# Who issues a 2 KB transfer: the shift row moves from SyncE's queue to ScalarE's, and its copies ahead of two exps

## The reference

```python
def _L0_conv_ref(x, Wq, bq, Wk, bk, Wv, bv):        # B=8, C=512, S=1024 tokens, 8 heads of 64
    t = x.reshape(B, C, S).transpose(0, 2, 1)
    q = t @ Wq.T + bq ; k = t @ Wk.T + bk ; v = t @ Wv.T + bv
    q = q.reshape(B * NUM_HEADS, S, hd)             # k and v likewise
    scores = jnp.einsum('gqd,gkd->gqk', q, k) / jnp.sqrt(hd)
    attn = jax.nn.softmax(scores, axis=-1)
    wv = jnp.einsum('gqk,gkd->gqd', attn, v)
...
x = x + _L0_conv_ref(_gn(x), ...)                   # _gn: group norm, 32 groups
x = x + _L1_conv_ref(_gn(x), ...)                   # mask, relu, 3x3 convolution, bias
```

## Time and profile before

| what | us |
| --- | --- |
| median of 3 runs (lowest, highest) | 2591.8 (2591.47, 2593.41) |
| the profiled execution | 2588.92 |
| its span, first to last instruction | 2587.1 |
| 100 to 1480 us, attention in its regular part: PE busy / DVE busy / ACT busy of 1380 | 1356.72 / 1092.56 / 760.76 |
| 1480 to 1830 us, attention's last slots, with the convolution's preparation | PE busy 326.88 of 350 |
| 1830 to 2587 us, convolution | PE busy 745.40 of 757 |

### The profile page before, as it was taken

How to read it: one execution, slowest core, us unless ns; L and a number is a source line. 1 busy time by engine, 2 the same in 40 slices (tenths; PEclk the granted TensorE clock), 3 DMA queues, 4 the chain that set the end, 5 groups by cost and what they waited for, 6 DMA issues and landing times.

```text
span 2587.1 us, 39690 instructions
## 1 busy us (share of the span) xinstructions
PE 2499.2 (97%) x11720; PEld 986.9 (38%) x11720; DVE 1936.6 (75%) x2647; ACT 1141.9 (44%) x2059; POOL 1124.8 (43%) x971
## 2 busy tenths in 40 slices
PE   6899999999999999999999999988999999999998
PEld 2333333333333333333333333332444444444443
DVE  5877787878788787887878888887676967967415
ACT  4455555455555555555555554456232132132100
POOL 1466467457556646655655664554112021030000
PEclk9999999999999999999999999999999999999999
DMA  5324243251433415323243332511444634633533
GB/s 159 84 71 118 69 128 87 61 138 55 123 84 98 117 44 130 102 69 106 71 122 83 109 106 58 136 48 60 173 177 152 238 133 176 228 130 131 209 113 149
DMA packets 209643, 300.66 MB, mean 116 GB/s; under 512 B 82192, under 2 KB 131472, under 8 KB 209424
## 3 DMA queue, kind: packets, MB, share of 16 engines
q1 hardware_dynamic: 209424, 297.97, 38.7%
HBM read 194.49 MB, written 52.69 MB: 96 GB/s over the span
## 4 chain that ended last, share of the span: by engine, by line
PE 86%; DVE 6%; issue 2%; ACT 2%; DMA 2%; POOL 1%; SPq 0%; DVEq 0%; ACTq 0%; POOLq 0%
PE bank L835 27%; PE bank L741 16%; PE bank L715 15%; PE bank L676 12%; PE bank L694 8%; PE bank L686 6%; DVE nmax L1264 2%; PE bank L704 1%; DMA q_b<-shift 1%; ACT prob L918 1%; DVE prob_sum L1258 1%; DVE bn L220 1%; PE bank L728 0%; DVE val L1276 0%; DVE xn L1334 0%
## 5 line engine op out<-in xcount | busy, mean ns | idle before, releaser
L1264 DVE TENSOR_REDUCE nmax<-bank 128x1 f32<-128x512 f32 x1024 | 657.6, 681 | 230.5 <-PE bank L694 226.2
L918 ACT ACTIVATE prob<-bank 128x512 f32<-128x512 f32 x1024 | 560.5, 593 | 502.7 <-PE bank L715 502.3
L835 PE MATMUL bank<-v,u_slab 128*128 128x512 f16 x3456 | 746.9, 379 | 0.0
L1093 POOL TENSOR_TENSOR prob_sum<-prob_sum,prob 128x512 f32<-128x512 f32 x354 | 504.6, 1425 | 369.0 <-ACT prob L918 368.1
L741 PE MATMUL bank<-prob,val 128*64 128x512 f32 x2048 | 495.9, 605 | 0.0
L835 PEld LDWEIGHTS bank<-v,u_slab 128*128 128x128 f16 x3456 | 338.1, 98 | 406.9 <-issue 0.8
L694 PE MATMUL bank<-k_a,q_a 128*128 128x512 f16 x1024 | 384.7, 383 | 18.4 <-DVE nmax L1264 10.3
L1258 DVE TENSOR_TENSOR prob_sum<-prob_sum,prob 128x512 f32<-128x512 f32 x354 | 353.4, 998 | 3.5 <-issue 0.3
L715 PE MATMUL bank<-q_a,k_a 128*128 128x512 f16 x1024 | 315.6, 381 | 18.0 <-ACT prob L918 16.4
L715 PE MATMUL bank<-q_b,k_b 128*128 128x512 f16 x1024 | 306.2, 381 | 9.5 <-DMA q_b<-shift 9.5
L741 PEld LDWEIGHTS bank<-prob,val 128*64 128x64 f32 x2048 | 124.1, 136 | 248.7 <-issue 206.8
(11 more groups left out here) (139 smaller groups left out, 2512.1 us busy)
## 6 DMA issues: line engine op xcount, KB each, us to landing
u_slab<-u_scratch SPq DMA_DIRECT2D x72, 1024.0 KB, 5.0
xs<-x SPq DMA_DIRECT2D x28, 1024.0 KB, 5.7
tile<-x_scratch SPq DMA_DIRECT2D x26, 1024.0 KB, 5.9
u_scratch<-u_w SPq DMA_DIRECT2D x96, 192.0 KB, 2.7
q_a<-qk_hi SPq DMA_DIRECT2D x64, 256.0 KB, 4.9
den_sb<-recip_scratch SPq DMA_DIRECT2D x128, 128.0 KB, 2.9
x_scratch<-xr SPq DMA_DIRECT2D x16, 1024.0 KB, 4.5
xr<-x SPq DMA_DIRECT2D x15, 1024.0 KB, 7.7
```

The source lines that it names most:

```text
L835: mm = pe.matmul(bank_at(pos, co)[:].rearrange("p (i n) -> p i n", i=2), slab[:, l, c, co * P:(co + 1) * P], image[v][:, 2 * c:2 * c + 2, ...
L918: act.activation(prob[:, (2 * u + e) % 8], sc_bank[bank_turn(s * 16 + 2 * u + e, 16 * HPI)[0]][:], ACT.Exp, scale=float(D) ** -0.5).then_i ...
L1093: nc.gpsimd.tensor_tensor(acc, in0, prob[:, (2 * kc + 1) % 8], ALU.add).then_inc(s1["sum1"], 1)
L1264: dve.tensor_reduce(nmax[:, m // 2, m % 2:m % 2 + 1], src[:], AX.X, ALU.max, negate=True)\
```

## The change

The transfer of the shift row is no longer issued by SP but by ACT, from its own DMA queue, right behind the four copies and after a wait for them (`shift_sent`). `send_shift` is gone. Beside that the copies, and with them the new wait and the new issue, move: where the slot has r < 3 they stand ahead of both exps of unit 6, where r = 3 they stay between them.

```diff
-            def send_shift(h, s):
-
-                half, tok = tokens(s)
-                sp.wait_ge(s1["shift_sent"], TOK // SQ * (h + 1))
-                sp.dma_start(q_b[half][D:D + 1, :, tok], shift[:]).then_inc(s1["shift_row"], 16)
...
-                if nxt:
-                    send_shift(img * HPI + s + 1, (s + 1) % HPI)
...
-            def gather_shift(h, first=False):
+            def gather_shift(h, s, first=False):
...
+                half, tok = tokens(s)
+                act.wait_ge(s1["shift_sent"], TOK // SQ * (h + 1))
+                act.dma_start(q_b[half][D:D + 1, :, tok], shift[:]).then_inc(s1["shift_row"], 16)
...
+                    if nxt and u == UNITS - 2 and r < HPH - 1:
+                        gather_shift(h + 1, (s + 1) % HPI)
                     exp_tile(h, s, u, 0, added)
-                    if nxt and u == UNITS - 2:
-                        gather_shift(h + 1)
+                    if nxt and u == UNITS - 2 and r == HPH - 1:
+                        gather_shift(h + 1, (s + 1) % HPI)
                     exp_tile(h, s, u, 1, added)
```

More of the change, by code:

```diff
@@ L559, in _ @@
             load_x(1, 0)
-            send_shift(0, 0)
             slot(0, 0, prev=False)
@@ L1045, in _ @@
                 qk_evacuate(1, 0, j)
-            gather_shift(0, first=True)
+            gather_shift(0, 0, first=True)
             slot(0, 0, prev=False)
```

## The result

| | before | changed |
| --- | --- | --- |
| median of the runs made together (lowest, highest) | 2592.45 us (2591.47, 2593.41), 4 runs | 2611.37 us (2609.9, 2614.28), 4 runs |
| again, with more rounds | 2591.34 us (2589.69, 2594.66), 9 runs | 2610.97 us (2610.12, 2613.9), 5 runs |
| span of the profiled execution | 2587.1 us | 2609.8 us |

The ratio is 1.0072 with a 95% interval of 1.006 to 1.0084, and 1.0078 (1.0064 to 1.0091) the second time: the change makes the kernel 19 to 20 us slower. The forecast was slower by 26, 2618 us, with a range of 2602 to 2632 that holds the result.

A forecast was written before the change was run, and what follows sets the result against it. The prediction took PE, busy 97% of the span, as the bound. Its terms, 25.2 + 0.3 + 1.5 + 3 - 3.5 = +26.5 us on 2588.9, gave 2615.4, with 2.9 for the median 2618 us, range 2602 to 2632.

The forecast's parts named there:

- part 3: Slots 0, 1, 4, 5: copies and issue delay unit 6's first exp, stalling PE in unit 7, 29 times, 25.2 us.
- the 2.9 us that were added for the median: Whole kernel: the median of the runs lies 2.9 us above the profiled execution, so 2615.4 became 2618 us.
- PE is busy without a gap behind it, so nothing gives it back: Behind unit 7's stalls projections follow, so all 29 count in full: 18.9 + 6.3 = 25.2 us.
- Part 1: Start of slot 2: off SP's queue, the shift row lands sooner and PE waits less, gain 3.5 us, bounds 2 and 5.4.
- rival (b): Unit 6: issue and sequencer's rows take under 0.1 us, PE never waits; 2588 us, 0.15% faster; chance 0.04.
- Part 5: Slots with r = 3: the issue ahead of unit 6's second exp costs 0.1 us or so each, 15 slots, 1.5 us.
- Part 6: Last image, slots 3 to 6: late shift blocks and ACT's mask work cost 3 us together, bounds 1 and 6.
- (a): Unit 6: the issue holds ACT for 0.1 us or so, stalls near 0.2 us; +5.0, 2597 us; chance 0.08.
- (d): Unit 6: ACT's issue is of the short kind, 0.40 us; +14.7, 2606.5 us, slower all the same; chance 0.20.
- Rival (c): Slots with filter stores: SP and ACT issues collide, 22 slots cost up to 0.4 more; +9, 2627 us; chance 0.13.

The follow-up runs named there:

- Experiments 1: Changed kernel with the copies back between the exps of unit 6 in every slot, ACT still issuing: 2596.61 us against 2593.43 for the kernel before, ratio 1.0015.
- experiment 2: Kernel before with only the copies moved ahead of unit 6's exps where r < 3, SP issuing: 2593.74 us against 2593.43, ratio 1.0001.
- 4: Changed kernel with the wait for the copies and ACT's issue moved behind both exps of unit 6: 2591.6 us against 2593.43 for the kernel before, ratio 0.9998.
- experiment 3: Changed kernel with the shift row sent as two half-length transfers, each issued by ACT: 2643.93 us against 2593.43 for the kernel before, ratio 1.0195.
- 6: Changed kernel with SP's 1 MB load of slot 1 waiting for the shift row's landing: 2612.02 us against 2593.31 for the kernel before, ratio 1.0069.
- experiment 5: Kernel before with SP issuing slot 1's shift row ahead of load and first store: 2589.05 us against 2593.31, ratio 0.9985; with copies ahead too: 2589.68, 0.9992.

## Why the prediction was right, point by point

**The sign and the place (part 3) were right.** The stall is where it was put, in unit 7 of slots 0, 1, 4 and 5, for the exp that was named. Experiments 1, 2 and 4 take away one thing each (the copies ahead of both exps, the issuer, the issue ahead of the exps) and each takes away the loss but for 3 to 5 us at most, and experiment 3, with a second issue, raises it to 50 us. The working stands on a slack of 1.10 us against 1.95 us of new work, and 1.92 was measured.

**Its size was right, 24.5 us for 25.2, in part by luck.** In the 24 regular slots 20.9 were forecast and 20.0 found. The term that was mis-sized there is the issue, 0.73 taken from SP's rows: on ACT it is 0.63 to 0.67 in slots of this kind; the sequencer's rows behind it made up part of that with 0.25 for 0.22. The last five slots, which I took to be like the others, give 4.5 for 4.3 only because one of them, with late blocks of the shift, has 1.61.

**The total, 26 forecast and 20 measured, was too large for what the sum left out.** In the profiles the loop's jump gives 2.1 us back and shorter waits of PE another 1.6 in the last two images; neither is in the sum. The clock, which nearly cancels between the two traces, was not in it either. And the 2.9 us that were added for the median are the distance of one quick execution of before; the changed kernel's profiled execution (2611.67 us) lies at its median (2611.37).

**"PE is busy without a gap behind it, so nothing gives it back" was wrong in one place.** Five of the stalls lie in slot 0 just ahead of the loop's jump. There the gap at the jump shrank by 0.2 to 0.6 us each, in sum 2.1 us: the changed kernel has 3.8 us of it where before had 5.9. Over all kernels of this study the sum at the jump is 2.9 to 4.0 with the stalls (changed kernel twice, experiments 3 and 6) and 4.6 to 6.4 without them. That the stalls shorten it is likely and not shown for each gap: experiment 2, without these stalls, has 4.6, which is 1.3 less than before. What the jump waits for no row shows.

**Part 1 had the right number for the wrong reason.** "With a queue of its own the row should land sooner" failed: it landed in 5.4 to 6.2 us into slot 2, later if anything, and the issue row and PE's wait in the image of the earlier trace rows show it:

```profile
565.92 0.67 ACTq L922
...
572.21 0.61 PE L706 MATMUL bank<-q_b,k_b 128*128 128x512 f16 x2 [0.45 <-DMA q_b<-shift]
```

Part of the delay may also be SP's second filter store; no run separates it from the load. I wrote that it waits for POOL anyway; it had waited behind the shift row, and now leaves with the first, just as ACT issues:

```profile
564.75 0.38 SPq L456 DMA_DIRECT2D xs<-x  x1
565.41 1.09 SPq L445 DMA_DIRECT2D u_scratch<-u_w  x2
```

The waits for the row shrank by 4.1 us although it landed no sooner: PE itself came 0.75 us later to them, as the text on rival (b) said in passing. In experiments 1 and 2, where PE is not late, they are 10.8 us. The page "DMA: Bandwidth & Descriptors" of the Trainium skill (section "Issuing engines are not separate DMA queues") had this right, and experiments 1 and 6 agree with it: 5.0 to 5.7 us on ACT's queue beside the load, 1.73 without it. I cited it and gave it no weight in the forecast's own term; it should have stood there.

And DVE's part of that term was too small: not three of the seven waits ahead of slot 2 are worth nothing, but all six in the regular images, as experiment 5 shows.

**Part 5** expected 0.1 us in each of 15 slots and got 2.0 us in another way: 13 slots at 0.05 or less, and 0.86 and 0.91 in slots 3 and 7 of the image before the last. There the shift's blocks come late, so that the issue falls where no cover is left. ACT and PE there, in slot 3:

```profile
1504.79 0.98 ACT L918 ACTIVATE shift<-shift_blk 8x32 f16<-8x32 f32 x4 [0.92 <-DVE shift_blk L1268]
1505.81 0.63 ACTq L922 DMA_DIRECT2D q_b<-shift  x1
1506.56 1.58 ACT L909 ACTIVATE prob<-bank 128x512 f32<-128x512 f32 x3 [0.78 <-PE bank L706]
...
1507.21 0.88 PE L706 MATMUL bank<-q_a,k_a 128*128 128x512 f16 x2 [0.70 <-ACT prob L909]
```

**Part 6** was right in kind and nearly in size: 5.0 us for 3, inside its bounds, and some 3.5 without the clock. In slot 6 the stall is 2.1 us where 1.6 to 1.8 were expected. Beside the earlier trace rows, the copies now wait 3.07 us ahead of both exps, and unit 7's exps start at 1825.25, 21.1 us later than before, where the attention already stood 18.7 later at the slot's start:

```profile
1820.44 0.98 ACT L918 ACTIVATE shift<-shift_blk 8x32 f16<-8x32 f32 x4 [3.07 <-DVE shift_blk L1268]
1821.45 0.66 ACTq L922 DMA_DIRECT2D q_b<-shift  x1
...
1825.25 1.07 ACT L909 ACTIVATE prob<-bank 128x512 f32<-128x512 f32 x2
```

Of the rivals, (a), (b) and (d) needed a short issue and are out with 64 of 0.63 us and more. Rival (c) is out too: 17 of ACT's issues overlapped one of SP's in time and took 0.63 to 0.69 us, the same as the others.

## What to carry to other kernels

A DMA issue costs the issuing engine's sequencer two thirds of a microsecond here, and what it costs the kernel is decided by what stands behind it: put it behind the work that others wait for, and behind an instruction long enough to cover it, and it is free. Before two things are moved ahead of an instruction, add them up against its one slack. A small transfer that someone waits for belongs ahead of large ones in time, since another issuer's queue does not pass them by; and a wait taken away is worth only what the next late engine leaves of it.

## What the runs showed that I had not expected

- On ACT the issue takes 0.627 to 0.692 us (1.22 the first time), on SP 0.677 to 0.798 for the same transfer, and two issuers at once did not slow each other.
- A 2 KB transfer on ACT's queue lands 1.73 us after its issue when SP's 1 MB load waits for it, and 5.4 to 6.2 us after it when the load and two stores of 192 KB had been or were being issued by SP within the 1.2 us around it.
- PE's gap at the loop's jump is not a constant: 0.3 to 2.1 us each, and in sum shorter in the kernels in which PE had been held in unit 7 just before.
- Single stretches in which PE's granted clock fell to half speed lie in different places in each trace, and one of them cost 1.69 us in a busy place. The granted clock over the whole run, 0.993 to 0.997, goes with most of the 10 us by which executions of one kernel differ.
